# Two self attentions with the last values projected one step later, and a reordered end of the program, in a two-layer decoder on one core

## The chip, the cores and the metric

The kernel runs on one core of a Trainium2 chip. The metric is the device time of one execution in microseconds (us), the median of several runs. The engines are named as the profile names them: PE is TensorE (matmuls and transposes), PEld its weight loads, DVE VectorE, ACT ScalarE, POOL GpSimd, SP SyncE, which here issues nearly all transfers (SPq in the trace).

## The reference, cut to what matters

The input x has 8 batches of 128 tokens of 512 values. It goes through six blocks, each added to x and followed by a layer norm:

```
x = LN(x + attn0(x))            # 32 heads of 16, causal, biases
x = LN(x + autocorrelation(x, ctx))
x = LN(x + experts_lora(x))     # 28 experts, top 2
x = LN(x + attn1(x))            # 32 heads, clipped qkv, LN of q and k, ALiBi
x = LN(x + cross_attention(x, ctx))   # 16 heads, 4 groups of keys
x = LN(x + routed_lora(x))      # 8 heads of rank 16, softmax router
```

The change touches the two self attentions (`attn0`, `attn1`) and the last block of the last two pairs of batches. In an attention `v = x Wv` weighs nothing until the probabilities of its batch are known; only the product of probabilities and values needs it.

## The kernel before, in words

Everything is one program, with an instruction order written out by hand for every engine and semaphores between the engines. An engine takes its instructions strictly in that order.

**Self attentions.** Each of the two (`l` = 0 and 1) runs over steps `i`, four to a batch: batch `b = i // 4`, phase `r = i % 4`. The function `attention_step(l, i)` exists once for each engine. In every step PE makes the scores of step `i` twice: for the row maxima (into `s_bank`, L870, with the causal mask added on L844) and, five steps later and turned over, for the exponentials (into `t_bank`, L875). DVE reduces the first (`maxima`, L2134), ACT takes the exponential of the second (`probs`, L1406). PE's `scores(l, i)` waits for DVE's maxima of step `i - 1` and for ACT's exponentials of step `j - 1`, where `j = i - 5`. In the phases 1 and 3 PE multiplies probabilities and values (`weigh_values`, L891).

Beside these, the table `M_STEP` says which other product goes into which phase, and `M_BATCH` for which batch: phase 0 has the turned maxima, the rows of x, the output projection `o` and the transpose of q (`qT`); phase 1 has the projection of v of batch `b` and then the transpose of k of batch `b + 1` (`kT`, L829); phases 2 and 3 have the projections of q and k of batch `b + 2`, which the last two batches (6 and 7) no longer have. A projection is 12 matmuls of 512 columns (L749 to L751). All of them take turns in two banks of PSUM, `m_bank`; the order in `m_uses` decides which, and `bank_taken(u)` makes PE wait until the use before the last has been read.

After `kT`, ACT copies the turned keys into the ring `qk` (`qk_split`; one instruction for each of two halves in layer 0, L1374; eight smaller ones in layer 1, L1378). Then SP writes the extra rows of the keys and queries (`extra_rows`, L668, eight transfers), and PE's scores at the first step of the next batch (phase 0) wait for them. In its own order ACT has, in step `4b + 1`: `probs`, then the first half of a weight split (`split_hi`, L1339); in step `4b + 2`: `qk_split` of the keys, then `probs`. DVE takes v out of PSUM (`values`, L2089 in layer 0, L2091 in layer 1) at the head of the step behind the one that projects it. The turned maxima of a batch (L837) go to ACT and by SP's L659 into `qk`.

**End of the program.** Batches go in four trips of two (slots `s` = 0 and 1). The last block of trip 2 (`routes_and_low`, `low_to_rank`, `heads_out`) is woven into the cross attention of trip 3, and the last block of trip 3 stands alone at the end. All its products are in `bank[s][2]`: first 136 columns of router logits and low ranks (L1161), then the transpose (L1166), then 512 columns of output (L1172). DVE has `routes` (L2370 to L2372), `routed` (L2378 to L2380), `ff_add` (L2385) and `ff_moments` (L2390 to L2393); POOL makes rstd and shift (L1837, L1840); ACT applies them (`ff_norm`, L1613) and SP stores the batch when `ff_ready` says so. `norm_x_of_cross` (L2402) is the norm behind the cross attention, on DVE; `cross_add` is L2216 and `cross_moments` L2223 to L2227, with its rstd on POOL's L1826.

Of the kernel before, what the change touches and what calls it, by code (L numbers as in the profile page):

```python
# [109 lines left out]
def decoder(nc, a, out):  # L110
# [9 lines left out]
    with es:  # L120
# [174 lines left out]

        def bank_of_xv(trip, s, n):

            return bank[1][0] if (trip, s, n) == (0, 1, 0) else bank[s][3]
# [179 lines left out]
        M_STEP = (("max", "x", "o", "qT"), ("v", "kT"), ("q",), ("k",))  # L478
        M_BATCH = {"max": -1, "x": 2, "o": -3, "qT": 1, "v": 0, "kT": 1, "q": 2, "k": 2}

        def of_step(i, kind):

            b = i // STEPS + M_BATCH[kind]
            return b if kind in M_STEP[i % STEPS] and 0 <= b < B else None

        m_uses = {}
        for l in range(2):
            for i in range(FIRST, LAST):
                for kind in M_STEP[i % STEPS]:
# [125 lines left out]
        def _(sp):  # L615
# [18 lines left out]
            def store(trip, s):  # L634
                sp.wait_ge(ff_ready, row_of(trip, s))
# [108 lines left out]
        def _(pe):  # L744
# [411 lines left out]
            def routes_and_low(trip, s):  # L1156
# [3 lines left out]
                for k in range(KT):  # L1160
                    ins = mm(bank[s][2][:, 0:NL], plain_hT[:, k, s, 1, :], w_al[:, k, :], start=k == 0, stop=k == KT - 1)  # L1161
                ins.then_inc(mix_psum, 1)

            def low_to_rank(trip, s):
                pe.wait_ge(mixed_ready, mix(trip, s, FF))
                nc.tensor.transpose(bank[s][2][:, 0:P], low[s], ident[:, :]).then_inc(mixedT_psum, 1)  # L1166

            def heads_out(trip, s):
# [3 lines left out]
                mm(bank[s][2][:, :], plain_hT[:, KT - 1, s, 0, :], w_bl, start=True, stop=True).then_inc(ff_psum, 1)  # L1172
# [97 lines left out]
            for trip in range(TRIPS):  # L1270
# [26 lines left out]
                if behind:  # L1297
                    each(heads_out, trip - 1)
                cross_out(trip, 1, XKV - 1)
            x_to_features(TRIPS - 1, 0, FF, 1)  # L1300
            pe.wait_ge(ff_added, row_of(TRIPS - 2, 0))
# [3 lines left out]
            pe.wait_ge(ff_added, row_of(TRIPS - 2, 1))  # L1305
# [6 lines left out]
        def _(act):  # L1312
# [293 lines left out]
            def low_copied(trip, s):  # L1606
                act.wait_ge(mixedT_psum, mix(trip, s, FF))
                copy(plain_hT[:, KT - 1, s, 0, :], bank[s][2][:, 0:P]).then_inc(low_ready, 1)
# [126 lines left out]
            each(ff_norm, TRIPS - 1)  # L1735

        @block.gpsimd
        def _(pool):
# [95 lines left out]
            def ff_rows(trip, s):  # L1834
# [6 lines left out]
                                        ).then_inc(ff_rstd, 1)  # L1841

# [185 lines left out]
            each(ff_rows, TRIPS - 1)  # L2028

        @block.vector  # L2030
        def _(dve):
# [335 lines left out]
            def routes(trip, s):  # L2367
                dve.wait_ge(mix_psum, mix(trip, s, FF))
                e = st[s][:, EIGHT]
                steps_done(FF, trip, v.tensor_tensor(e, bank[s][2][:, LH * LR:NL], br_row[:, :], ALU.add))  # L2370
# [3 lines left out]
            def routed(trip, s):  # L2374
# [5 lines left out]
                v.tensor_tensor(low[s].rearrange("p (h r) -> p h r", h=LH), bank[s][2][:, 0:LH * LR].rearrange("p (h r) -> p h r", h=LH),  # L2380
                                e.unsqueeze(2).broadcast_to([P, LH, LR]), ALU.mult).then_inc(mixed_ready, 1)

            def ff_add(trip, s):
                dve.wait_ge(ff_psum, row_of(trip, s))
                v.tensor_tensor(xb(trip, s), bank[s][2][:, :], xb(trip, s), ALU.add).then_inc(ff_added, 1)  # L2385
# [9 lines left out]
            def each(step, trip, *args):  # L2395
                for s in both:
                    step(trip, s, *args)

# [115 lines left out]
            cross_moments(TRIPS - 1, 0)  # L2514
# [63 lines left out]
```

## Time and profile before

| | |
|---|---|
| median of 3 runs | 920.09 us (919.88 to 921.89) |
| profiled execution, own time | 921.42 us |
| its span, first to last instruction | 919.6 us |
| busy: PE, DVE, ACT, POOL | 855.2, 597.6, 419.6, 265.4 us |
| mean granted clock of TensorE | 0.98 |

The profiled execution is one run of the program; its span leaves out about 1.8 us around the first and last instruction, and its own time is 1.3 us above the median. A row of a timeline gives the start of an instruction (or of a few of the same kind), how long it took, its engine, line, operation and operands, and in brackets how long the engine sat idle before it and what it waited for. A row of a table of stretches gives the busy time of each engine in a stretch, the number of instructions, the granted clock (1.00 is full) and the share of the transfers.

### The profile page before, as it was taken

How to read it: one execution, taken by the hardware profiler on the slowest of the kernel's cores; microseconds unless marked ns; L12 is line 12 of the kernel's file. 1: busy time of each engine (PE TensorE's matmuls, PEld its weight loads, DVE VectorE, ACT ScalarE, POOL GpSimd, SP SyncE). 2: the span in 40 equal slices, each digit the busy share in tenths (PEclk: the TensorE clock that was granted, in tenths of full speed). 3: DMA queues.
4: the chain of work that ended last, by engine and by line, in shares of the span. 5: the costliest groups of instructions: out<-in, count | busy, mean ns of one | idle time of the engine just before them, and what ended most of it. 6: DMA issues, size and time to landing. Idle time of an engine off the chain costs nothing.

```text
span 919.6 us, 22457 instructions
## 1 busy us (share of the span) xinstructions
PE 855.2 (93%) x9192; PEld 692.4 (75%) x9192; DVE 597.6 (65%) x1526; ACT 419.6 (46%) x1078; POOL 265.4 (29%) x316
## 2 busy tenths in 40 slices
PE   6999998897997989899999798999999999999995
PEld 5777776674554777677777687888999898989983
DVE  3555665467896576567776543997377747665776
ACT  4354434344554334255555353543555364526532
POOL 1122222275985641101233246760000100010001
PEclk9999999999999999899999899999999999999998
DMA  6400000132231110000000011230000010000001
GB/s 225 159 20 15 20 16 23 60 93 81 80 100 36 46 40 4 9 27 17 17 17 17 26 36 57 88 122 8 24 1 2 1 47 1 2 2 24 2 2 46
DMA packets 21237, 37.11 MB, mean 40 GB/s; under 512 B 3264, under 2 KB 7488, under 8 KB 20880
## 3 DMA queue, kind: packets, MB, share of 16 engines
q1 hardware_dynamic: 21088, 35.62, 12.7%
q8 instruction: 73, 1.20, 0.5%
q14 instruction: 28, 0.23, 0.1%
q10 hardware_dynamic: 48, 0.07, 0.0%
HBM read 29.16 MB, written 2.10 MB: 34 GB/s over the span
## 4 chain that ended last, share of the span: by engine, by line
PE 73%; DVE 16%; issue 4%; POOL 2%; ACT 2%; DMA 2%; SPq 1%; POOLq 0%; DVEq 0%; ACTq 0%
PE bank L749 17%; PE bank L751 15%; PE bank L750 15%; PE bank L870 6%; PE bank L1142 4%; PE bank L891 3%; DVE tank L2348 3%; PE bank L844 2%; DVE tank L2358 2%; PE bank L875 2%; DVE tank L2263 1%; DVE tank L2134 1%; PE bank L829 1%; PE bank L1005 1%; PE bank L768 1%
## 5 line engine op out<-in xcount | busy, mean ns | idle before, releaser
L749 PE MATMUL bank<-wr,hTl 128*128 128x512 f32 (+3 forms) x472 | 190.6, 404 | 4.7 <-DVE wr L2063 2.3
L751 PE MATMUL bank<-wr,hTh 128*128 128x512 f32 (+3 forms) x472 | 181.5, 384 | 0.0
L750 PE MATMUL bank<-wr,hTh 128*128 128x512 f32 (+3 forms) x472 | 181.2, 384 | 0.0
L2134 DVE TENSOR_REDUCE tank<-bank 128x4 f32<-128x512 f32 x128 | 82.4, 686 | 57.0 <-PE bank L844 57.0
L749 PEld LDWEIGHTS bank<-wr,hTl 128*128 128x128 f32 (+1 forms) x472 | 90.3, 191 | 28.6 <-issue 8.6
L1406 ACT ACTIVATE pT<-bank 128x512 f32<-128x512 f32 x128 | 70.0, 605 | 88.1 <-PE bank L844 88.1
L751 PEld LDWEIGHTS bank<-wr,hTh 128*128 128x128 f32 (+1 forms) x472 | 90.0, 191 | 17.5
L750 PEld LDWEIGHTS bank<-wr,hTh 128*128 128x128 f32 (+1 forms) x472 | 90.4, 192 | 15.5 <-issue 1.2
L870 PE MATMUL bank<-qk 32*128 32x128 f32 x1024 | 75.5, 286 | 19.3 <-DVE tank L2134 8.8
L870 PEld LDWEIGHTS bank<-qk 32*128 32x128 f32 x1024 | 63.4, 188 | 35.9 <-issue 25.0
L875 PE MATMUL bank<-qk 32*128 32x128 f32 x1024 | 75.1, 285 | 0.3 <-DMA qk<-tank 0.3
L749 PE MATMUL bank<-hTh,wr 128*128 128x256 f32 (+1 forms) x240 | 73.3, 305 | 1.5 <-DVE hTl L2319 1.5
L751 PE MATMUL bank<-hTh,wr 128*128 128x256 f32 (+1 forms) x240 | 72.9, 304 | 0.0
L750 PE MATMUL bank<-hTl,wr 128*128 128x256 f32 (+1 forms) x240 | 72.9, 304 | 0.0
L1591 ACT ACTIVATE tank<-bank,stats 128x256 f32<-128x256 f32 x128 | 58.8, 482 | 23.2 <-DVE stats L2342 23.2
L875 PEld LDWEIGHTS bank<-qk 32*128 32x128 f32 x1024 | 62.7, 187 | 4.0 <-issue 3.0
L1378 ACT ACTIVATE qk<-bank,qk_shift,qk_scale 128x128 f32<-128x128 f32 x128 | 46.6, 474 | 24.7 <-PE bank L829 24.7
L2341 DVE TENSOR_REDUCE stats<-bank 128x2 f32<-128x512 f32 x64 | 43.8, 684 | 18.6 <-PE bank L751 18.6
L1837 POOL TENSOR_TENSOR stats<-stats,half 128x1 f32<-128x1 f32 x8 | 4.4, 550 | 175.4 <-DVE stats L2393 175.4
L2348 DVE COPY tank<-bank 128x512 f32<-128x512 f32 x64 | 39.7, 682 | 21.9 <-PE bank L1126 21.9
L1599 ACT CAST hTh<-bank 128x384 fp32r<-128x384 f32 x32 | 15.3, 479 | 83.4 <-PE bank L1142 83.4
L1142 PE MATMUL bank<-tank 128*32 128x128 f32 x1536 | 46.9, 280 | 2.8 <-DVE tank L2348 1.9
(238 smaller groups left out, 1854.3 us busy)
## 6 DMA issues: line engine op xcount, KB each, us to landing
raw<-w_qkv_dram SPq DMA_DIRECT2D x12, 256.0 KB, 2.9
raw<-w_xq_dram SPq DMA_DIRECT2D x16, 192.0 KB, 2.4
raw<-w_xo_dram SPq DMA_DIRECT2D x12, 256.0 KB, 2.8
x_all<-x_dram SPq DMA_DIRECT2D x8, 256.0 KB, 6.4
cin<-ctx_dram SPq DMA_DIRECT2D x8, 256.0 KB, 2.9
cin<-ctxT_dram SPq DMA_DIRECT2D x8, 256.0 KB, 2.9
out_dram<-x_all SPq DMA_DIRECT2D x8, 256.0 KB, 2.0
qk<-extra_dram SPq DMA_DIRECT2D x124, 16.0 KB
```

Of the source, the lines that this page charges most:

```text
L749: mm(dst, lhs[1], rhs[0], start=start, stop=False)
L750: mm(dst, lhs[0], rhs[1], start=False, stop=False)
L751: return mm(dst, lhs[0], rhs[0], start=False, stop=stop)
L870: ins = mm(s_bank[n][:, at], qk[b % RING][g, e, m, :], qk[b % RING][g, 2 + e, m, :], start=m == 0, stop=True, skip_group_check=True)
L875: ins = mm(t_bank[n][:, at], qk[c % RING][g, 2 + f, m, :], qk[c % RING][g, f, m, :], start=m == 0, stop=True, skip_group_check=True)
L1142: ins = mm(bank[s][0][row:row + NARROW, tile * P:(tile + 1) * P], xv[s][:, at:at + NARROW], xpT[s][:, (2 * j + t) * P:(2 * j + t + 1) * P] ...
L1378: ins = av(qk[b % RING][:, 2 * i + e, m, :], m_bank[u % 2][:, m * P:(m + 1) * P], ACT.Identity, bias=qk_shift[:, i, e, m:m + 1], scale=qk_ ...
L1406: av(pT[e][:, 2 * rows + n, :], t_bank[n][:, :], ACT.Exp).then_inc(exp_ready, 1)
L1591: ins = av(xp[s][:, h * XT:(h + 1) * XT], bank[s][i][:, j * XT:(j + 1) * XT], ACT.Exp, bias=st[s][:, NEGMAX.start + h:NEGMAX.start + h + 1 ...
L2134: v.tensor_reduce(nm[b % 2][:, at:at + KT], s_bank[n][:, :].rearrange("p (m t) -> p m t", m=KT), AX, ALU.max, negate=True).then_inc(max_re ...
L2341: steps_done(XA, trip, v.tensor_reduce(r, bank[s][i][:, :].rearrange("p (h t) -> p h t", h=2), AX, ALU.max))
L2348: v.tensor_copy(xpT[s][:, i * 512:(i + 1) * 512], bank[s][i][:, :]).then_inc(xpT_ready[s], 1)
```

## The change

In both self attentions, for batches 6 and 7 alone, phase 1 keeps only `kT` and the projection of v goes to phase 2, where these batches have nothing else; the use of the two banks follows that order, and DVE's `values` follows one step later.

At the end of the program, for trip 3 the products of the last block go to `bank[s][0]`. The two `heads_out` of trip 2, which stood before the output projection of slot 1 in the cross attention of trip 3, stand behind both output projections. PE's two waits for `ff_added` of trip 2 go. DVE's order is changed: slot 1 of the cross attention is added and measured before the `ff_add` of trip 2, and those and their moments are spread further back. The very last norm (trip 3, slot 1) goes from ACT to DVE, in the form with mean and rstd (`last_norm`), so POOL makes rstd alone for it (`ff_last`), and the last store waits for DVE.

```diff
+        def ff_bank(trip, s):
+            return bank[s][2] if trip + 1 < TRIPS else bank[s][0]
...
         M_STEP = (("max", "x", "o", "qT"), ("v", "kT"), ("q",), ("k",))
+        M_STEP_AT_END = (("max", "x", "o", "qT"), ("kT",), ("v",), ())
+        def kinds(i):
+            return (M_STEP_AT_END if i // STEPS in (B - 2, B - 1) else M_STEP)[i % STEPS]
...
-            return b if kind in M_STEP[i % STEPS] and 0 <= b < B else None
+            return b if kind in kinds(i) and 0 <= b < B else None
...
             def store(trip, s):
-                sp.wait_ge(ff_ready, row_of(trip, s))
+                if (trip, s) == (TRIPS - 1, 1):
+                    sp.wait_ge(ff_added, row_of(trip, s) + 1)
+                else:
+                    sp.wait_ge(ff_ready, row_of(trip, s))
...
                 cross_out(trip, 0, XKV - 1)
-                if behind:
+                if more and behind:
                     each(heads_out, trip - 1)
                 cross_out(trip, 1, XKV - 1)
+            each(heads_out, TRIPS - 2)
             x_to_features(TRIPS - 1, 0, FF, 1)
-            pe.wait_ge(ff_added, row_of(TRIPS - 2, 0))
             routes_and_low(TRIPS - 1, 0)
             x_to_features(TRIPS - 1, 1, FF, 1)
             low_to_rank(TRIPS - 1, 0)
-            pe.wait_ge(ff_added, row_of(TRIPS - 2, 1))
             routes_and_low(TRIPS - 1, 1)
...
             ff_norm(TRIPS - 2, 1)
-            each(ff_norm, TRIPS - 1)
+            ff_norm(TRIPS - 1, 0)
...
+            def ff_last(trip, s):
+                pool.wait_ge(ff_var, row_of(trip, s))
+                _, mv, rs, _ = ff_slots(trip)
+                nc.gpsimd.tensor_tensor(st[s][:, rs], st[s][:, mv][:, 1:2], half[:, 0:1], ALU.pow).then_inc(ff_rstd, 1)
...
             each(ff_rows, TRIPS - 2)
-            each(ff_rows, TRIPS - 1)
+            ff_rows(TRIPS - 1, 0)
+            ff_last(TRIPS - 1, 1)
...
+            def last_norm(trip, s):
+                _, mv, rs, _ = ff_slots(trip)
+                dve.wait_ge(ff_rstd, row_of(trip, s, 2, 1))
+                v.tensor_scalar(xb(trip, s), xb(trip, s), st[s][:, mv][:, 0:1], st[s][:, rs], ALU.subtract, ALU.mult).then_inc(ff_added, 1)
...
             cross_add(TRIPS - 1, 0)
             cross_moments(TRIPS - 1, 0)
+            cross_add(TRIPS - 1, 1)
+            norm_x_of_cross(TRIPS - 1, 0)
+            cross_moments(TRIPS - 1, 1)
             ff_add(TRIPS - 2, 0)
-            norm_x_of_cross(TRIPS - 1, 0)
+            norm_x_of_cross(TRIPS - 1, 1)
+            routes(TRIPS - 1, 0)
             ff_add(TRIPS - 2, 1)
-            cross_add(TRIPS - 1, 1)
-            cross_moments(TRIPS - 1, 1)
-            routes(TRIPS - 1, 0)
-            norm_x_of_cross(TRIPS - 1, 1)
             routed(TRIPS - 1, 0)
             ff_moments(TRIPS - 2, 0)
             routes(TRIPS - 1, 1)
+            ff_moments(TRIPS - 2, 1)
+            routed(TRIPS - 1, 1)
             ff_add(TRIPS - 1, 0)
-            routed(TRIPS - 1, 1)
-            ff_moments(TRIPS - 2, 1)
             ff_moments(TRIPS - 1, 0)
             ff_add(TRIPS - 1, 1)
             ff_moments(TRIPS - 1, 1)
+            last_norm(TRIPS - 1, 1)
```

## Rows read from the trace of the kernel before

**Rows 1.** Stretches of 6 and 5 us, layer 0 and layer 1, around step 28.

```profile
162.00:168.00 6.00, 5.88 (x60) 4.45 (x60) 1.29 (x2) 1.08 (x2) 0.00 (x0) 0.72 0.31 93
...
514.00:519.00 5.00, 5.00 (x51) 3.93 (x45) 1.29 (x2) 1.09 (x2) 0.00 (x0) 0.66 0.15 41
```

**Rows 2.** Timeline, layer 0, steps 25 to 28: PE, ACT, SP.

```profile
150.09 0.50 PE L749 MATMUL bank<-wr,hTl 128*128 128x512 f32 x1
...
153.00 0.60 PE L829 MATMUL bank<-ident,tank 128*128 128x128 f32 x4
...
156.32 0.38 PE L870 MATMUL bank<-qk 32*128 32x128 f32 x2 [1.28 <-DVE tank L2134]
...
162.12 0.38 PE L870 MATMUL bank<-qk 32*128 32x128 f32 x2 [2.69 <-DMA qk<-extra_dram]
...
153.63 1.45 ACT L1374 ACTIVATE qk<-bank,small_sb 128x512 f32<-128x512 f32 x2 [3.05 <-PE bank L829]
...
155.11 5.34 SPq L668 DMA_DIRECT2D qk<-extra_dram  x8
```

**Rows 3.** Timeline, layer 0, steps 29 to 32: DVE, PE.

```profile
173.59 0.76 DVE L2089 TENSOR_TENSOR tank<-bank,tank 128x256 f32<-128x256 f32 x2
...
176.13 0.88 DVE L2154 TENSOR_TENSOR tank<-tank,scratch 128x256 f32<-128x256 f32 x2
...
177.72 1.29 DVE L2134 TENSOR_REDUCE tank<-bank 128x4 f32<-128x512 f32 x2
...
176.27 0.38 PE L870 MATMUL bank<-qk 32*128 32x128 f32 x2 [1.28 <-DVE tank L2134]
...
179.06 0.33 PE L837 MATMUL bank<-ident,tank 128*128 128x128 f32 x1 [0.28 <-DVE tank L2134]
```

**Rows 4.** Timeline, layer 1, steps 25 to 28: PE, ACT, SP.

```profile
502.88 0.60 PE L829 MATMUL bank<-ident,tank 128*128 128x128 f32 x4
...
507.54 0.38 PE L870 MATMUL bank<-qk 32*128 32x128 f32 x2 [2.63 <-ACT pT L1406]
...
513.47 0.38 PE L870 MATMUL bank<-qk 32*128 32x128 f32 x2 [1.61 <-issue]
...
500.39 1.13 ACT L1406 ACTIVATE pT<-bank 128x512 f32<-128x512 f32 x2
501.34 0.57 ACT L1339 CAST wr<-raw 128x384 fp32r<-128x384 f32 x1
503.51 2.91 ACT L1378 ACTIVATE qk<-bank,qk_shift,qk_scale 128x128 f32<-128x128 f32 x8 [1.60 <-PE bank L829]
...
506.45 5.37 SPq L668 DMA_DIRECT2D qk<-extra_dram  x8
```

**Rows 5.** Timeline, end of the program, to the last routed low ranks: DVE, PE.

```profile
899.18 1.88 PE L1172 MATMUL bank<-raw,plain_hT 128*128 128x512 f32 x4
...
903.20 0.69 DVE L2216 TENSOR_TENSOR x_all<-bank,x_all 128x512 f32<-128x512 f32 x1
...
906.03 0.54 DVE L2402 TENSOR_SCALAR x_all<-x_all,stats 128x512 f32<-128x512 f32 x1
...
906.58 0.17 DVE L2378 RECIPROCAL stats<-stats 128x1 f32<-128x1 f32 x1
...
910.72 0.15 DVE L2378 RECIPROCAL stats<-stats 128x1 f32<-128x1 f32 x1
...
908.05 1.17 PE L1161 MATMUL bank<-raw,plain_hT 128*128 128x136 f32 x8 [0.33 <-ACT plain_hT L1322]
```

**Rows 6.** Timeline, end of the program, the last moments and norm.

```profile
912.39 0.68 DVE L2390 BATCH_NORM_STATS2 stats<-x_all 128x6 f32<-128x512 f32 x1
...
915.30 0.55 POOL L1837 TENSOR_TENSOR stats<-stats,half 128x1 f32<-128x1 f32 x1 [0.74 <-DVE stats L2393]
916.02 0.27 POOL L1840 TENSOR_SCALAR stats<-stats 128x1 f32<-128x1 f32 x1 [0.17 <-POOL stats L1837]
916.32 0.81 ACT L1613 ACTIVATE x_all<-x_all,stats 128x512 f32<-128x512 f32 x1 [0.92 <-POOL stats L1840]
```

More of the change, by code:

```diff
@@ L488, in decoder @@
             for i in range(FIRST, LAST):
-                for kind in M_STEP[i % STEPS]:
+                for kind in kinds(i):
                     if of_step(i, kind) is not None:
@@ L1160, in routes_and_low @@
                 for k in range(KT):
-                    ins = mm(bank[s][2][:, 0:NL], plain_hT[:, k, s, 1, :], w_al[:, k, :], start=k == 0, stop=k == KT - 1)
+                    ins = mm(ff_bank(trip, s)[:, 0:NL], plain_hT[:, k, s, 1, :], w_al[:, k, :], start=k == 0, stop=k == KT - 1)
                 ins.then_inc(mix_psum, 1)
@@ L1165, in low_to_rank @@
                 pe.wait_ge(mixed_ready, mix(trip, s, FF))
-                nc.tensor.transpose(bank[s][2][:, 0:P], low[s], ident[:, :]).then_inc(mixedT_psum, 1)
+                nc.tensor.transpose(ff_bank(trip, s)[:, 0:P], low[s], ident[:, :]).then_inc(mixedT_psum, 1)
             def heads_out(trip, s):
@@ L1171, in heads_out @@
                     pe.wait_ge(raw_loaded[1], loaded_piece(PIECES_REST + 1, 0, 0, PIECES_XV))
-                mm(bank[s][2][:, :], plain_hT[:, KT - 1, s, 0, :], w_bl, start=True, stop=True).then_inc(ff_psum, 1)
+                mm(ff_bank(trip, s)[:, :], plain_hT[:, KT - 1, s, 0, :], w_bl, start=True, stop=True).then_inc(ff_psum, 1)
             def each(step, trip, *args):
@@ L1607, in low_copied @@
                 act.wait_ge(mixedT_psum, mix(trip, s, FF))
-                copy(plain_hT[:, KT - 1, s, 0, :], bank[s][2][:, 0:P]).then_inc(low_ready, 1)
+                copy(plain_hT[:, KT - 1, s, 0, :], ff_bank(trip, s)[:, 0:P]).then_inc(low_ready, 1)
             def ff_norm(trip, s):
@@ L2369, in routes @@
                 e = st[s][:, EIGHT]
-                steps_done(FF, trip, v.tensor_tensor(e, bank[s][2][:, LH * LR:NL], br_row[:, :], ALU.add))
+                steps_done(FF, trip, v.tensor_tensor(e, ff_bank(trip, s)[:, LH * LR:NL], br_row[:, :], ALU.add))
                 steps_done(FF, trip, v.tensor_reduce(st[s][:, ONE_C], e, AX, ALU.max))
@@ L2379, in routed @@
                 steps_done(FF, trip, v.tensor_scalar(e, e, st[s][:, ONE_C], LH * 32.0 / LR, ALU.mult, ALU.mult))
-                v.tensor_tensor(low[s].rearrange("p (h r) -> p h r", h=LH), bank[s][2][:, 0:LH * LR].rearrange("p (h r) -> p h r", h=LH),
+                v.tensor_tensor(low[s].rearrange("p (h r) -> p h r", h=LH),
+                                ff_bank(trip, s)[:, 0:LH * LR].rearrange("p (h r) -> p h r", h=LH),
                                 e.unsqueeze(2).broadcast_to([P, LH, LR]), ALU.mult).then_inc(mixed_ready, 1)
@@ L2384, in ff_add @@
                 dve.wait_ge(ff_psum, row_of(trip, s))
-                v.tensor_tensor(xb(trip, s), bank[s][2][:, :], xb(trip, s), ALU.add).then_inc(ff_added, 1)
+                v.tensor_tensor(xb(trip, s), ff_bank(trip, s)[:, :], xb(trip, s), ALU.add).then_inc(ff_added, 1)
             def ff_moments(trip, s):
```

## The prediction

> **What bounds the kernel now.** I read the page first. PE is busy 855 of 919.6 us and is the last thing waited for nearly everywhere, so a stall counts only where PE stands idle, or where PE runs at half clock; the mean granted clock is 0.98, so that is rare. Then I went to the places of the change in the timeline, engine by engine, and looked for PE's idle time in brackets. It is in the steps that the change touches: batches 6 and 7 have no q or k to project in phases 2 and 3, so PE has nothing there but the scores, and waits for the answers to them. In layer 0 PE waits 1.28 us for DVE's maxima before the scores of step 27 and 2.69 us for the extra rows before those of step 28 [rows 2]; for batch 7 again 1.28 us before step 31, and 0.28 us before the turned maxima [rows 3]. In layer 1 it waits 2.63 us for ACT at step 27 and 1.61 us before step 28 [rows 4], where "issue" stands for the same transfers: SP issues them until 511.82, and 1.65 us later PE goes on, as in layer 0 (160.45 and 162.12). Last, the chain at the end of the program [rows 5, 6].
>
> **Layer 0, batch 6.** The keys' path to step 28 is a chain: the transposes start at 153.00, ACT copies 153.63 to 155.08, SP issues eight transfers in 5.34 us from 155.11, and PE starts step 28 at 162.12 [rows 2]: 9.1 us, none of it waiting for another engine. Now v stands behind it. v's twelve matmuls take from 150.09 to 153.00 [rows 2], so the chain starts 2.91 us earlier. Nothing else holds it: ACT and SP are idle then (ACT has waited 3.05 us for these transposes [rows 2]; the cast before it ends inside that wait), and the bank that the transposes now take is that of `o` of batch 3, read by DVE before v begins. PE has room to be ready at 159.2: it had 1.28 + 2.69 = 3.97 us of idle time, and v moves into it with 2.91. Term: 2.9 us. Bounds: 1.3 (only the maxima's wait is filled) and 4.0 (all idle time gone).
>
> **Layer 0, the clock.** Behind the 2.69 us wait the granted clock falls to 1.2 GHz, 0.72 on average over 162 to 168 [rows 1], while PE is busy 5.88 of 6 us. Lost: 6.0 x 0.28 = 1.7 us; the scores of step 28 are partly issue-bound, so I take 1.5. With about 1.3 us of idle time left, in two short pieces, that stretch looks like steps 29 to 32, where waits of 1.28 and 0.28 us [rows 3] were followed by no fall. Term: 1.5 us, bounds 0 and 1.7. The Trainium skill (TensorE: Matmul & The Clock Gate, "Loop structure matters more than you think") says that waiting for a DMA between matmuls makes the clock drop and that matmuls back to back keep it up; by that rule the stretch keeps its full clock, and the trace agrees in where the clock fell.
>
> **Batch 7, both layers.** No transpose here, only v moved from step 29 to 30. PE's 1.28 us wait before step 31 [rows 3] goes, since v lies between; a short new one comes before step 30, whose scores now follow `weigh_values` directly: the same sequence ends in 0.28 us before L837 [rows 3]. That would leave 1.0. But DVE is the next limit. It was free of step 29's work when it took v at 173.59 [rows 3]; now the maxima of step 30 start there and end at 174.9 (1.29). Then `weighed` for 1.6 us (176.13 to 177.72 [rows 3]), to 176.5, then v for 0.76, to 177.2, and only then the maxima of step 31, which PE's next instruction waits for. They started at 177.72 [rows 3]. Gain 0.5 to 0.7; I take 0.65 for each layer, bounds 0 and 1.28. In layer 1 the rows repeat this to 0.01 us. Queued behind DVE's delay are only later moments, with slack.
>
> **Layer 1, batch 6.** Transposes 2.91 us earlier again, from 502.88 to 499.97 [rows 4]. But ACT is not free: the exponentials of step 20 run until 501.52 and the cast `split_hi` until 501.91 [rows 4], and the keys' split is behind both in ACT's order. So it starts at 501.9 in place of 503.51, 1.6 earlier; from there to step 28 is 9.96 us (503.51 to 513.47 [rows 4]), so step 28 starts at 511.9. PE gets a new wait, for the exponentials before the scores of step 26: from 500.5 to 501.55, 1.0 us. It costs nothing by itself, as PE then comes to step 28 at 509.1 and still waits 2.8 us for the transfers. Term: 1.6 us, bounds 0.6 and 2.9. The clock was down before and behind step 28 (0.66 over 514 to 519 [rows 1], 5.0 x 0.34 = 1.7 us lost). As 2.8 us of waiting stay in front of the same place, I let this loss stand: term 0, bounds 0 and +1.7.
>
> **What follows** starts from those times: the transfers, splits and copies behind both attentions are released by the last steps' own results, none by something older that is still running. The values of both batches are needed only by `weigh_values` a step or more later, the wait for them on the bank's next user is over by then. So gains pass on whole.
>
> **The end.** The four matmuls of both `heads_out` of trip 2 (1.88 us as shown, 1.7 of them PE's alone [rows 5]) stood between the output projections and go behind the second, PE's sum unchanged. So DVE's add of slot 1 starts 1.7 earlier than 903.20, and its norm about 1.5 earlier than 906.03 [rows 5]. What is late next: `routed` of slot 0, which could start at 906.58 [rows 5] and now has an `ff_add` of 0.69 before it, from which 0.4 lies in idle time and 0.3 delays it. `low_to_rank` of slot 0 waits for it, and L1161 of slot 1 is behind that in PE's order: about 907.85 against 908.05 [rows 5]. Then trip 2's `ff_moments` of slot 1 (1.1 us, as 912.39 [rows 6] and the two small ones behind it) stands before `routed` of slot 1, which therefore starts at 910.65 against 910.72 [rows 5]. Of the 1.7 us, 0.1 stays. Behind that slot 0's add and moments end about 0.2 before the last `ff_add` needs DVE, so they cost nothing. The last norm: POOL's 0.55 stays; its second operation and ACT's 0.81, which ended at 917.13 [rows 6], give way to DVE's form of the same shape, 0.54 [rows 5], from 915.9 to 916.45. That is 0.65 to 0.7. The last store waits only for this; the one before it is issued 1.4 us earlier. The other bank and the two waits taken away are worth nothing: the wait seen there is for ACT's copy, 0.33 [rows 5]. Term: 0.75, bounds 0.3 (DVE's queue eats the rest) and 1.4 (the moved moments fall into idle time).
>
> **Sum.** 2.9 + 1.5 + 0.65 + 1.6 + 0.65 + 0.75 = 8.05 us. The profiled execution, 921.4, would come to 913.4; it is 1.3 above its median, so the median comes from 920.1 to 912.0.
>
> **Rivals.** (a) One half-clock stretch less: the one of layer 1 goes too; 910.4. For it: first idle 1.0, then 2.8, not 2.63 and 1.61. Against: 2.69 before the fall in layer 0. Chance 0.13. (b) The fall in layer 0 stays, or another comes in its place further on, for the autocorrelation has waits of its own; 913.5. Chance 0.17. (c) The transfers do not follow the transposes, because SP's or ACT's queue holds them: only the maxima's waits go, 1.3 + 0.65 in layer 0, 0.6 + 0.65 in layer 1, and 0.75: 4 us, 916. Against: SP is idle before both L668 rows. Chance 0.10. (d) The new waits eat it all, PE idles in other places by as much: 920. It needs a bound behind the attentions (weights, POOL) that I did not find. Chance 0.05. (e) Slower: everything behind step 25 shifts against the clock's control, and half-clock stretches fall on more busy places. Each costs up to 1.7 us [rows 1]; it decides from five net more, 8.05 / 1.7, and then gives 922. For it: waits of 1.0 and 2.8 us in layer 1 are new. Against: the mean clock is 0.98 in a program that already has waits of 1 to 3 us. Chance 0.04. The forecast itself has 0.51.
>
> **How the numbers follow.** The range reaches over (a) and (b) and into (c): 909 to 916. A change of 0.2% (1.84 us) is about what a measurement of this kernel can tell. Faster by more: the forecast, (a), (b), (c), 0.91; within it: (d), 0.05; slower: (e), 0.04.
>
> **What would show it.** In the changed profile: in layer 0 about 9.1 us from the transposes of the keys to step 28, a wait below 1.1 us before it and full clock behind it; layer 1's keys' split directly behind the cast L1339, a PE wait near 1 us before step 26 and near 2.8 us before step 28; before step 31 no wait, and DVE's v right before its maxima; at the end POOL's last operation followed by DVE's, then the store. Wrong if PE still waits over 2 us before step 28 in layer 0, if the autocorrelation takes longer than before by some us, or if the last norm ends less than 0.3 or more than 1.4 us earlier, counted from the last L1142.

## The result, and the profile after

The changed kernel takes 912.22 us (median of 10 runs, 908.46 to 916.69), the kernel before on the same chip 920.37 us (10 runs, 919.21 to 923.38): a ratio of 0.9904, 95% interval 0.9883 to 0.9925. The forecast was 912.0, in a range of 909 to 916. The profiled execution took 912.89 us (forecast 913.4), with a span of 911.1, 8.5 below that of before. So "faster" was right, and nearly to the microsecond; the steps behind the sum were not all of the size that they were given, and part of the agreement is luck: errors of about 1 us each that cancel. None of the signs that were to show the forecast wrong appeared.

In the code of after the lines named here stand 11 to 18 further down: L870 is L882, L837 is L849, L829 is L841, L875 is L887, L2134 is L2151, L2089 is L2106, L1172 is L1184. The first view is the timeline of the changed kernel in layer 0, steps 25 to 32, to be held beside [rows 2, 3]:

```profile
151.23 0.66 PE L841 MATMUL bank<-ident,tank 128*128 128x128 f32 x4
...
159.04 0.33 PE L849 MATMUL bank<-ident,tank 128*128 128x128 f32 x1 [0.27 <-DVE tank L2151]
160.42 0.38 PE L882 MATMUL bank<-qk 32*128 32x128 f32 x2 [1.05 <-DMA qk<-extra_dram]
...
164.85 0.38 PE L882 MATMUL bank<-qk 32*128 32x128 f32 x2
...
167.64 0.38 PE L882 MATMUL bank<-qk 32*128 32x128 f32 x2 [0.27 <-DVE tank L2151]
...
174.86 0.33 PE L849 MATMUL bank<-ident,tank 128*128 128x128 f32 x1 [0.27 <-DVE tank L2151]
...
151.93 1.45 ACT L1385 ACTIVATE qk<-bank,small_sb 128x512 f32<-128x512 f32 x2 [0.21 <-PE bank L841]
...
153.40 5.34 SPq L680 DMA_DIRECT2D qk<-extra_dram  x8
...
170.18 1.22 DVE L2151 TENSOR_REDUCE tank<-bank 128x4 f32<-128x512 f32 x2
...
172.87 0.71 DVE L2106 TENSOR_TENSOR tank<-bank,tank 128x256 f32<-128x256 f32 x2
173.51 1.29 DVE L2151 TENSOR_REDUCE tank<-bank 128x4 f32<-128x512 f32 x2
```

The turned keys leave PE at 151.23 and the scores of step 28 start at 160.42, 9.19 us later; the transfers take the same 5.34 us, and PE's wait is down from 2.69 to 1.05 us. The waits of 1.28 us before steps 27 and 31 are gone; 0.27 before step 30 (167.64) is new. DVE takes v at 172.87, directly behind `weighed`, and its maxima of step 31 follow at 173.51.

Layer 1, steps 25 to 32, beside [rows 4]:

```profile
494.17 0.66 PE L841 MATMUL bank<-ident,tank 128*128 128x128 f32 x4
495.85 0.38 PE L882 MATMUL bank<-qk 32*128 32x128 f32 x2 [1.02 <-ACT pT L1417]
...
503.07 0.33 PE L849 MATMUL bank<-ident,tank 128*128 128x128 f32 x1 [0.28 <-DVE tank L2151]
506.03 0.58 PE L882 MATMUL bank<-qk 32*128 32x128 f32 x2 [2.63 <-DMA qk<-extra_dram]
...
513.07 0.38 PE L882 MATMUL bank<-qk 32*128 32x128 f32 x2
...
515.86 0.38 PE L882 MATMUL bank<-qk 32*128 32x128 f32 x2 [0.27 <-DVE tank L2151]
...
523.08 0.33 PE L849 MATMUL bank<-ident,tank 128*128 128x128 f32 x1 [0.27 <-DVE tank L2151]
...
495.53 0.57 ACT L1350 CAST wr<-raw 128x384 fp32r<-128x384 f32 x1
495.93 2.97 ACT L1389 ACTIVATE qk<-bank,qk_shift,qk_scale 128x128 f32<-128x128 f32 x8
...
498.93 5.37 SPq L680 DMA_DIRECT2D qk<-extra_dram  x8
```

The keys' split stands right behind the cast, as forecast, with the new wait for ACT (1.02 us) and 2.63 us of waiting for the transfers. The clock is in the table of stretches (columns as in [rows 1]), three rows of after:

```profile
162.00:168.00 6.00, 5.73 (x104) 4.42 (x108) 3.55 (x6) 2.65 (x5) 0.00 (x0) 1.00 0.42 134
506.00:512.00 6.00, 5.97 (x56) 4.90 (x57) 1.29 (x2) 1.08 (x2) 0.00 (x0) 0.51 0.11 34
904.00:905.00 1.00, 1.00 (x2) 0.20 (x2) 0.82 (x3) 0.56 (x1) 0.02 (x1) 0.71 0.18 66
```

and one more of before, in layer 1, behind the wait of 2.63 us in front of step 27:

```profile
506.00:512.00 6.00, 4.32 (x81) 3.44 (x81) 2.89 (x6) 3.10 (x8) 0.30 (x1) 0.72 0.07 19
```

Behind layer 0's step 28 the granted clock stays at 1.00, where it was 0.72, and PE does 104 matmuls in 6 us instead of 60 [rows 1] (the same six microseconds, but not the same steps; step 28 itself took 4.43 us in place of 5.92). Behind layer 1's it is 0.51, the lower of the two levels (1.2 GHz) for nearly all of the six microseconds, deeper than the 0.66 of before [rows 1]. The third row is in the last product. The end of the program, beside [rows 5, 6]:

```profile
889.03 0.44 PE L1178 MATMUL bank<-ident,tank 128*128 128x128 f32 x2
...
898.25 0.68 DVE L2403 TENSOR_TENSOR x_all<-bank,x_all 128x512 f32<-128x512 f32 x1
898.85 0.15 DVE L2395 RECIPROCAL stats<-stats 128x1 f32<-128x1 f32 x1
...
902.42 0.15 DVE L2395 RECIPROCAL stats<-stats 128x1 f32<-128x1 f32 x1
...
908.04 0.55 DVE L2421 TENSOR_SCALAR x_all<-x_all,stats 128x512 f32<-128x512 f32 x1 [0.67 <-POOL stats L1857]
...
899.82 1.09 PE L1173 MATMUL bank<-raw,plain_hT 128*128 128x136 f32 x8
...
903.90 1.61 PE L1184 MATMUL bank<-raw,plain_hT 128*128 128x512 f32 x2 [0.35 <-ACT plain_hT L1619]
```

To book the difference, both traces are parted at the same instructions. Rows of before that are used for it and were not shown yet: step 29 in both layers, the turned maxima at the end of layer 1's attention, and two places in the tail.

```profile
168.04 0.38 PE L870 MATMUL bank<-qk 32*128 32x128 f32 x2
...
519.42 0.38 PE L870 MATMUL bank<-qk 32*128 32x128 f32 x2
...
530.44 0.33 PE L837 MATMUL bank<-ident,tank 128*128 128x128 f32 x1 [0.28 <-DVE tank L2134]
...
896.74 0.44 PE L1166 MATMUL bank<-ident,tank 128*128 128x128 f32 x2
...
912.21 1.13 PE L1172 MATMUL bank<-raw,plain_hT 128*128 128x512 f32 x2 [0.35 <-ACT plain_hT L1608]
```

| stretch | before | after | gain | forecast |
|---|---|---|---|---|
| start to the end of step 25's products of values, layer 0 | 150.09 | 151.23 | -1.1 | 0 |
| from there to step 28 | 12.03 | 9.19 | 2.8 | 2.9 |
| step 28 to the turned maxima, layer 0: clock | | | 1.5 | 1.5 |
| the same: v of batch 7 | | | 1.0 | 0.65 |
| to the same place of layer 1's step 25 (499.97; 494.17) | 320.9 | 319.3 | 1.6 | 0 |
| from there to step 28 | 13.50 | 11.86 | 1.6 | 1.6 |
| step 28 to the turned maxima, layer 1: clock | | | -1.1 | 0 |
| the same: v of batch 7 | | | 1.0 | 0.65 |
| to trip 2's last transposes (896.74; 889.03) | 366.3 | 365.95 | 0.35 | 0 |
| to the end of the last norm (917.13; 908.59) | 20.39 | 19.56 | 0.8 | 0.75 |

"Clock" and "v of batch 7" are parted at step 29: from step 28 to 29 layer 0 took 5.92 us before and 4.43 after, layer 1 5.95 and 7.04; from step 29 to the turned maxima both layers went from 11.02 to 10.01. The sum is 8.5 us. In the tail the last product starts 15.47 us behind the transposes before (896.74 to 912.21) and 14.87 after (889.03 to 903.90), but itself took 1.61 us against 1.13. Trip 2's transposes stand directly behind the last L1142, so the 0.8 us of the last row is also the distance that the forecast named for its end.

### The profile page after: what moved, and what is told of

Its sections match the earlier page's. It is cut to its first block, busy times and chain, and to the rows that moved or that the text cites. A ratio compares the mean times of both kernels' runs of the same rounds, so it can differ in the third digit from the quotient of the medians.

```text
span 911.1 us, 22453 instructions
## 1 busy us (share of the span) xinstructions
PE 852.5 (94%) x9192; PEld 689.2 (76%) x9192; DVE 599.0 (66%) x1527; ACT 418.0 (46%) x1077; POOL 264.9 (29%) x315
## 4 chain that ended last, share of the span: by engine, by line
PE 71%; DVE 17%; issue 4%; ACT 2%; DMA 2%; POOL 2%; SPq 2%; POOLq 0%; DVEq 0%; ACTq 0%
PE bank L761 17%; PE bank L762 15%; PE bank L763 15%; PE bank L882 6%; PE bank L1154 4%; DVE tank L2365 3%; PE bank L903 2%; PE bank L856 2%; DVE tank L2375 2%; PE bank L887 1%; DVE tank L2151 1%; PE bank L1017 1%; DVE tank L2280 1%; PE bank L841 1%; SPq L680 1%
## 5 line engine op out<-in xcount | busy, mean ns | idle before, releaser
L2151 DVE TENSOR_REDUCE tank<-bank 128x4 f32<-128x512 f32 x128 | 82.2, 683 | 52.6 <-PE bank L856 52.6
L882 PE MATMUL bank<-qk 32*128 32x128 f32 x1024 | 75.8, 286 | 13.9 <-DVE tank L2151 5.4
L882 PEld LDWEIGHTS bank<-qk 32*128 32x128 f32 x1024 | 63.7, 189 | 31.2 <-issue 23.6
L887 PE MATMUL bank<-qk 32*128 32x128 f32 x1024 | 75.2, 285 | 0.3 <-DMA qk<-tank 0.3
L887 PEld LDWEIGHTS bank<-qk 32*128 32x128 f32 x1024 | 62.9, 188 | 4.0 <-issue 3.0
L2375 DVE TENSOR_SCALAR tank<-tank,stats 128x256 f32<-128x256 f32 x128 | 47.6, 414 | 2.3
```

The source lines that it names most:

```text
L882: ins = mm(s_bank[n][:, at], qk[b % RING][g, e, m, :], qk[b % RING][g, 2 + e, m, :], start=m == 0, stop=True, skip_group_check=True)
L887: ins = mm(t_bank[n][:, at], qk[c % RING][g, 2 + f, m, :], qk[c % RING][g, f, m, :], start=m == 0, stop=True, skip_group_check=True)
L2151: v.tensor_reduce(nm[b % 2][:, at:at + KT], s_bank[n][:, :].rearrange("p (m t) -> p m t", m=KT), AX, ALU.max, negate=True).then_inc(max_re ...
L2375: ins = v.tensor_scalar(block, block, sums[:, j:j + 1], None, ALU.mult)
```

## The experiments

All ratios are to the kernel before, run on the same chip. Over all of them the kernel before had 75 runs, median 921.03 us, standard deviation 2.6; a median of 12 runs is therefore good to some 1 us, and the terms are read in the profiles as distances between two instructions, which repeat to 0.1 us where the clock is the same.

**The attentions alone.** The kernel before with the new table for batches 6 and 7, the end untouched.

```diff
+        M_STEP_AT_END = (("max", "x", "o", "qT"), ("kT",), ("v",), ())
+            return (M_STEP_AT_END if i // STEPS in (B - 2, B - 1) else M_STEP)[i % STEPS]
```

> Only the two self attentions are changed; the end of the program is that of the kernel before. Theory of the prediction: the gain is made of local terms, 2.8 (keys' path, layer 0) + 1.0 (batch 7, layer 0) + 1.6 (keys' path, layer 1) + 1.0 (batch 7, layer 1) = 6.4 us, and half-clock stretches move it by up to 1.7 us each either way: a median 5 to 8.5 us below the kernel before. In the profile, from the transposes of the keys of batch 7 to step 28: 9.2 us in layer 0 and 11.9 in layer 1. Rival (the gain is taken back behind the attentions by transfers and splits): under 3 us. Rival (the end does most of it): under 2 us.

Measured: 913.82 us (12 runs), 0.9922 (0.9893 to 0.9951). Layer 0 from the transposes of the keys to step 28 takes 9.14 us with a wait of 1.00, layer 1 11.89 us with 2.64, and the clock falls behind layer 1's step 28 as in the changed kernel (9.98 us from step 28 to 30, in full clock 7.2). So these distances belong to this half of the change, and most of the time does.

**Batch 7's v alone.**

```diff
-            return (M_STEP_AT_END if i // STEPS in (B - 2, B - 1) else M_STEP)[i % STEPS]
+            return (M_STEP_AT_END if i // STEPS in (B - 1,) else M_STEP)[i % STEPS]
```

> Only the values of batch 7 are projected one step later, in both layers; batch 6 and the end are those of the kernel before. Theory (each batch has its own wait): 1.0 us in each layer from the scores of step 29 to the turned maxima (11.02 us before, 10.0 here), the wait before step 28 stays at 2.69 us and the half clock behind it too; the median 2 us below the kernel before, plus or minus 1.5 for half-clock stretches. Rival (the gain is all that of batch 6, VectorE's queue bounds batch 7): under 0.5 us in the two stretches together.

Measured: 920.51 us, 0.9981 (0.9959 to 1.0004). Layer 0's waits at steps 27 and 28 are those of before (1.28 and 2.68 us), and in both layers the waits before step 31 are gone, with 10.0 us from step 29 to the turned maxima in place of 11.0. The local gain is 1.0 in each layer; the total, 0.6 us less, is at the low edge of what was expected and does not part the change from nothing.

**Batch 6's v alone.**

```diff
-            return (M_STEP_AT_END if i // STEPS in (B - 2, B - 1) else M_STEP)[i % STEPS]
+            return (M_STEP_AT_END if i // STEPS in (B - 2,) else M_STEP)[i % STEPS]
```

> Only batch 6's v is moved one step later, in both layers; batch 7's v and the program's end stay as before. Theory (the terms add up): L0 from the kT transposes to step 28 9.2 us instead of 12.0, the half clock behind step 28 gone (1.5), L1 from 13.5 to 11.9, a new half-clock stretch behind L1's step 28 (-1.1): 4.5 to 5 us in all, about 915.5. From the keys of batch 7 to the turned maxima the distance stays 11.0. Rival (batch 7's v, left where it was, gives part of it back, since its step starts earlier than its transfers land): L0's step 30 waits for the qk transfer, and the gain is 3 us or less, 917.5 or more.

Measured: 916.50 us (12 runs), 0.9945 (0.9922 to 0.9967): 4.9 us less. The timeline of this kernel, PE:

```profile
152.62 0.66 PE L834 MATMUL bank<-ident,tank 128*128 128x128 f32 x4
...
161.77 0.38 PE L875 MATMUL bank<-qk 32*128 32x128 f32 x2 [1.02 <-DMA qk<-extra_dram]
...
174.43 0.38 PE L875 MATMUL bank<-qk 32*128 32x128 f32 x2 [1.28 <-DVE tank L2139]
...
493.14 0.66 PE L834 MATMUL bank<-ident,tank 128*128 128x128 f32 x4
...
504.94 0.38 PE L875 MATMUL bank<-qk 32*128 32x128 f32 x2 [2.57 <-DMA qk<-extra_dram]
```

9.15 us in layer 0 and 11.80 in layer 1, the 1.28 before step 31 still there, and from step 28 to 31 12.66 us, against 14.15 before (162.12 to 176.27 [rows 2, 3]): 1.5 us is what the half clock behind the 2.69 us wait had cost. The rival, a wait at step 30 that eats part of it, did not come. Nor did the loss of 1.1 us that was expected behind layer 1's step 28: from there to step 29 it took 5.93 us, as before (5.95), though PE's wait was 2.57. So the distances add up to some 6 us, and the total has 4.9.

**The end alone**, that is, the changed kernel with the old table in both attentions.

```diff
-            return (M_STEP_AT_END if i // STEPS in (B - 2, B - 1) else M_STEP)[i % STEPS]
+            return (M_STEP_AT_END if False else M_STEP)[i % STEPS]
```

> Only the end of the program is changed, the attentions are those of the kernel before. Theory: 0.7 us from the last norm on VectorE and 0.1 to 0.6 from the order, a median 0.8 to 1.3 us below the kernel before, which is within what a measurement tells from nothing; in the profile 19.1 to 19.6 us from the last L1142-like product's transpose of the low ranks (trip 2) to the end of the last norm, against 20.39 before. Rival (the new order only shifts the queue on VectorE): 0.7 us or less, with the last heads_out no earlier.

Measured: 917.06 us, 0.9954 (0.9927 to 0.9981), 4 us less than the kernel before, where 0.8 to 1.3 were expected. The profile has only 1.3 of them at the end, 19.08 us from the transposes to the end of the norm in place of 20.39: the last product starts 14.88 us behind the transposes, as in the changed kernel, and the last norm is shorter. Up to the last 20 us the instructions are those of before, and layer 0's step 28 even was in half clock for longer (0.50 over 162 to 168, against 0.72 [rows 1]).

**The order of the end alone**: other bank and order, but the last norm on ACT as before.

```diff
-            last_norm(TRIPS - 1, 1)
...
-            ff_norm(TRIPS - 1, 0)
+            each(ff_norm, TRIPS - 1)
```

> The end of the program in its new order and with the other bank, but the last norm stays on ScalarE behind both GpSimd operations; attentions as before. Theory of the prediction: the order gives 0.1 us, the last norm 0.7, so this is 0.1 us below the kernel before. What the changed profile showed: the last heads_out starts 0.6 us earlier, counted from the transposes of trip 2's low ranks, so 0.6 us. Rival (the other bank matters by itself): a wait of TensorE for trip 2's adds appears nowhere in the kernel before, so nothing beyond the 0.6.

Measured: 919.97 us, 0.9972 (0.9950 to 0.9993). The last product again starts 14.87 us behind the transposes, 0.6 us earlier than before. Order, bank and the two waits taken away are not parted here.

**The last norm alone.** The kernel before with `ff_last` and `last_norm`, the old order and bank.

```diff
-            each(ff_norm, TRIPS - 1)
+            ff_norm(TRIPS - 1, 0)
...
-            each(ff_rows, TRIPS - 1)
+            ff_rows(TRIPS - 1, 0)
+            ff_last(TRIPS - 1, 1)
...
             ff_moments(TRIPS - 1, 1)
+            last_norm(TRIPS - 1, 1)
```

> Only the last norm goes from ScalarE to VectorE; the order of the end and all attentions as before. Theory: from the last sums on GpSimd to the end 0.7 us less, 919.7, a ratio of 0.999 whose interval can hold 1; the local distance in the profile decides. Rival (the gain of the two parts of the end comes only together, since the other bank is what frees VectorE): local distance unchanged.

Measured: 920.19 us, 0.9985 (0.9963 to 1.0007). From POOL's last operation (916.37) to the end of DVE's norm:

```profile
916.37 0.55 POOL L1849 TENSOR_TENSOR stats<-stats,half 128x1 f32<-128x1 f32 x1 [1.83 <-DVE stats L2402]
...
916.95 0.55 DVE L2412 TENSOR_SCALAR x_all<-x_all,stats 128x512 f32<-128x512 f32 x1 [0.67 <-POOL stats L1849]
```

1.13 us, against 1.83 before (915.30 to 917.13 [rows 6]). The 0.7 is there without the reordering, so the rival falls.

**The kernel before, again**, as a control of the comparison.

> The kernel before, unchanged, under another label: it measures what the comparison itself gives for no change. Theory (where the half-clock stretches fall differs from execution to execution, and the earlier single runs of the kernel before spread with a standard deviation of 2.6 us): a median within 2.5 us of the kernel before and an interval that holds 1. Rival (the comparison favours the kernel under test, so that part of the 8 us gained is not the change's): a median 3 us or more lower, a ratio below 0.997.

Measured: 920.93 us (12 runs), 1.0008 (0.9987 to 1.0030). The comparison favours nothing. In this execution the program's end was itself in half clock (0.73 over 904 to 909, where the first profile of before had 1.00), with no instruction changed.

**The changed kernel, again**, on the chip of the three that follow.

> The changed kernel itself, once more, beside the three built on it. Theory (half-clock stretches move the time from run to run): the single runs spread over 6 to 9 us, and within one kernel the longer runs are those with the lower mean clock, about 0.4 to 0.5 us for each us at half clock. The local stretches repeat to 0.1 us: 9.2 us and 11.9 us from the keys' transposes to step 28, 10.0 us from step 29 to the turned maxima. Rival (the spread comes from transfers): the runs' times have nothing to do with their clock.

Measured: 913.38 us (6 runs), 0.9928 (0.9901 to 0.9955). 9.16 us in layer 0; in layer 1 11.78, a wait of 2.54 and the same fall behind it (10.09 us from step 28 to 30).

**The wait filled.** Does layer 1's fall come from the wait for the transfers? Ten matmuls whose result nobody reads are put in front of step 28's scores in layer 1, into a bank that is free; the kernel computes all else as before.

```diff
+                if l == 1 and i == STEPS * (B - 1):
+                    u = m_uses[l, "o", b - 3]
+                    bank_taken(u)
+                    for _ in range(10):
+                        mm(m_bank[u % 2][:, :], w_qkv1[0][:, 0, 0:P], w_qkv1[0][:, 0, 0:D], start=True, stop=True)
                 scores(l, i)
```

> The changed kernel, with ten more matmuls of 512 columns in layer 1 between the turned maxima and the scores of step 28, written to a bank that the output projection overwrites: work without use, 2.3 us, inside the wait of 2.63 us. Theory (the half clock behind the wait comes from the wait): step 28 starts where it did, 11.9 us after the keys' transposes, and runs at full clock, 4.4 us to step 29 in place of 7.0; a median 1.5 to 2.6 us below the changed kernel although more is computed. Rival (the clock falls there for another reason, or falls later instead): step 28 as long as before, or the same sum with the fall in another place; then the time is that of the changed kernel. Rival (a cost of the added work): 0.2 us later.

Measured: 910.60 us (6 runs), 0.9899 (0.9879 to 0.9918). The timeline of PE and the table of stretches:

```profile
504.34 2.54 PE L932 MATMUL bank<-wr 128*128 128x512 f32 x10
507.18 0.38 PE L882 MATMUL bank<-qk 32*128 32x128 f32 x2 [0.31 <-issue]
...
514.41 0.38 PE L882 MATMUL bank<-qk 32*128 32x128 f32 x2 [0.27 <-DVE tank L2156]
```

```profile
507.00:513.00 6.00, 5.82 (x108) 4.62 (x108) 1.98 (x3) 1.09 (x2) 0.00 (x0) 1.00 0.13 37
```

Step 28 starts no earlier (11.84 us behind the transposes), but the clock behind it is 1.00 and step 30 follows 7.23 us later, in place of 9.83 (506.03 to 515.86). The fall did not move elsewhere nearby either: from 490 to 532 us the granted clock is 1.00 throughout. The fall was the wait's, and cost 2.6 us in this place. The medians on the same chip, 910.60 against 913.38, go the same way, though six runs of each would not show it alone. More work, less time.

**Two queues.** The eight transfers are issued one after another by SP in 5.3 us. Here, for the last batch, ACT's queue issues four of them, beside SP's four.

```diff
-                    if (l, b, e) != (0, 0, 0):
+                    if (l, b, e) != (0, 0, 0) and (b, e) != (B - 1, 1):
...
+                if i == STEPS * (B - 2) + 2:
+                    act.wait_ge(qk_rows, batch(l, B - 1, 2, 2))
+                    for g in range(GROUPS):
+                        at = g * PAD + 1
+                        act.dma_start(qk[(B - 1) % RING][at:at + 4, 1:4:2, :, :], a["extra"][l, 1, g]).then_inc(extra_loaded[1], 16)
```

> The changed kernel, but four of the eight transfers of the extra rows of batch 7 are issued by ScalarE, behind its exponentials of step 26, in both layers. Theory (what TensorE waits for at step 28 is the issue time of eight transfers one after another): the wait of 1.05 us in layer 0 goes, that of 2.63 us in layer 1 falls to about 0.6, step 28 starts 1.0 and 2.0 us earlier counted from the keys' transposes, and as the long wait is gone so is the half clock behind it in layer 1 (1.5 to 2.6 us): a median 3 to 5.5 us below the changed kernel. Rival (the waits are the landing time of the transfers or the split on ScalarE): less than 0.5 us in either layer. Rival (ScalarE's issue delays its exponentials and these TensorE): a new wait before step 27 or 29.

Measured: 905.97 us (4 runs, 903.61 to 907.86), 0.9848 (0.9824 to 0.9872), which is 7.4 us below the changed kernel on that chip, more than the expected 3 to 5.5. And once more, the same code:

> The changed kernel with the qk transfers of the last batches issued half on SyncE's queue and half on ScalarE's, the same code as the run at 905.97 us. Theory (the wait for the transfers behind the keys' transposes goes, 1.0 us in layer 0 and 2.0 in layer 1, and with it the half clock behind layer 1's step 28): 904 to 908 us, a ratio of 0.982 to 0.988. Rival (the earlier value was low because its half-clock stretches fell well by chance): 909 to 912, as the changed kernel less the local 3 us at most.

Measured: 910.82 us (6 runs, 905.41 to 911.38), 0.9875 (0.9848 to 0.9903), in the rival's range and not in the expected 904 to 908. So the first value was, in part at least, luck: by the clocks of the single runs, its four spent 24.9 us each at the lower level, the six of the second 31.5. The two were taken on different chips, and their intervals overlap. The timeline of the second, layer 0 and layer 1, and its stretch:

```profile
151.89 0.66 PE L841 MATMUL bank<-ident,tank 128*128 128x128 f32 x4
...
159.69 0.33 PE L849 MATMUL bank<-ident,tank 128*128 128x128 f32 x1 [0.27 <-DVE tank L2156]
159.95 0.38 PE L882 MATMUL bank<-qk 32*128 32x128 f32 x2
...
154.05 2.88 SPq L680 DMA_DIRECT2D qk<-extra_dram  x4
...
497.01 0.66 PE L841 MATMUL bank<-ident,tank 128*128 128x128 f32 x4
...
506.73 0.38 PE L882 MATMUL bank<-qk 32*128 32x128 f32 x2 [0.48 <-DMA qk<-extra_dram]
...
513.95 0.38 PE L882 MATMUL bank<-qk 32*128 32x128 f32 x2 [0.27 <-DVE tank L2156]
```

```profile
506.00:512.00 6.00, 5.51 (x89) 4.31 (x93) 1.98 (x3) 1.62 (x4) 1.27 (x1) 1.00 0.14 39
```

SP issues in 2.88 us what took 5.34; layer 0's step 28 comes 8.06 us behind the transposes without a wait for the transfers, layer 1's 9.72 us with 0.48, and the clock behind both is full. Locally that is 1.1 + 2.1 + 2.6 = 5.8 us less than the changed kernel. All ten runs of it have a median of 908.84 us, the sixteen of the changed kernel 912.88: a difference of 4.0 us, and it beats both kernels.

**Two queues, and the cast later.** The first half of layer 1's weight split stands before the keys' split on ACT; here, for step 25, it goes one step later, behind the keys' split and the exponentials, and ACT issues three transfers, SP five. The lines of the transfers are left out below.

```diff
-                if r == 1 and 0 <= b < B:
+                late = i - 1 if l == 1 and i in (STEPS * (B - 2) + 1, STEPS * (B - 2) + 2) else i
+                if (r == 1 and late == i or r == 2 and late < i) and 0 <= b < B:
                     split_hi(pieces(b // 2), b % 2, b // 2, 2, before)
```

> As the kernel with two queues, but five transfers are issued by SyncE and three by ScalarE, and in layer 1 ScalarE's weight cast of step 25 stands behind the keys' split and the exponentials of step 26. Theory (the keys' path is split, issue, landing, each behind the other): another 0.3 to 0.4 us earlier in layer 1 at the split, 11.9 us from the transposes to step 28 becomes 9.5 or less, so there is hardly a wait before step 28; a median 3.5 to 6 us below the changed kernel. Rival (the cast delayed holds the weights back later): a wait for weights behind the attention of layer 1 that the changed kernel does not have.

Measured: 909.34 us (6 runs), 0.9884 (0.9859 to 0.9909). PE and SP in layer 1:

```profile
504.88 0.50 PE L761 MATMUL bank<-wr,hTl 128*128 128x512 f32 x1 [0.83 <-POOL hTl L1802]
...
497.27 3.64 SPq L680 DMA_DIRECT2D qk<-extra_dram  x5
```

Layer 1 took 9.65 us from the transposes to step 28, where 9.5 or less was expected and 9.72 is the value with the cast in its place. The keys' split did start 0.4 us earlier behind the transposes (1.37 us in place of 1.77), but SP's issuing took 3.64 us in place of 3.01, so its last transfer went out no earlier. The two edits are not parted, and what the later cast gives with four transfers on either queue was not tried. Its price shows: 8.12 us (502.55 to 510.67) from step 28 to 30 in place of 7.22, with a new wait of 0.83 us, before the output projection, for a half of the attention's values (`hTl`) that POOL makes; in POOL's order it stands behind POOL's half of the weight split, which waits for the cast. The cast can't be delayed for nothing.

## Why the prediction came out right, point by point

**Layer 0, batch 6: right.** 2.84 us against 2.9, from one chain moved whole; alone (9.15 us) and in the changed kernel (9.19 and 9.16) it is the same. The rest of the wait, 1.05, is within what was said.

**Layer 0, the clock: right.** 1.5 us, and 1.00 over the stretch. The filled wait shows the mechanism in layer 1 by a direct test. The Trainium skill (TensorE: Matmul & The Clock Gate, "Loop structure matters more than you think") has matmuls back to back keep the clock up and a wait for a DMA between them lower it; the trace agrees with both halves, 1.00 with the wait filled and 0.51 with the wait.

**Batch 7: right mechanism, size too small.** I put 0.65 per layer and it gave 1.0. The step that was off is "DVE is the next limit ... now the maxima of step 30 start there", at 173.59. Counted from step 29's scores (168.04 before, 164.85 after), the maxima of step 30 started at 5.33 and not at the 5.55 where v had been taken, since they start right behind DVE's reciprocal; and maxima, multiplication, turn and v behind them took 3.33 (170.18 to 173.51) and not 3.6, as the rows' durations overlap by 0.05 to 0.1 us each. So the maxima of step 31 start at 8.66, where I had 9.16 and before had 9.68 (177.72 [rows 3]): 1.0 gained. That is the 1.0 that I had named as PE's own share, 1.28 less 0.27, and it is no coincidence: the maxima of step 31 start 1.44 us behind that step's first scores (172.07), as they do at step 27 (156.25 to 157.69), where DVE waits for the scores. So DVE only just keeps up, and PE's own order sets the distance, not DVE's queue.

**Layer 1, batch 6: right.** 1.64 against 1.6, with the cast as the limit and a new wait of 1.02 (forecast 1.0). In the experiment with the later cast the split does start 0.4 us earlier, which bears out the cast as the limit.

**Layer 1, the clock: wrong by 1.1.** The step that failed is "I let this loss stand". The wait did stay, 2.63, but the loss grew from 1.5 to 2.6 us (0.51 over the stretch instead of 0.66). The time at the lower level did not grow, it is some 7 us in both; its place changed. Before, one half of it (0.72 over 506 to 512) lay behind the wait in front of step 27 and cost nothing, as PE then waited 1.61 us for the transfers all the same; the other half (0.66 over 514 to 519) lay behind step 28. After, the wait in front of step 27 is gone, and nearly all of it (0.51 over 506 to 512, the rest in the wait of 2.63) lies behind step 28, where PE has no slack. Why one wait is followed by so long a fall is open, and it differs between profiles: it was so in three of the four in which batch 6's v is moved and the wait is left (the changed kernel twice, the attentions alone); with batch 6 alone it was half of that, 0.75 over 506 to 512, and cost 1.5. Of the six profiles in which batch 6 is as before, all have a fall behind the wait of 2.6 us in front of step 27, and five have one behind step 28, too. The sixth, with the last norm alone, has none there, although PE waited 1.65 us (12.66 us from step 28 to 31, against 14.18). This was neither rival (a) nor (e) but of their kind: one stretch more on a busy place.

**The end: right sum by luck, the order off.** The last norm gave 0.7 (forecast 0.65 to 0.7). The order gave 0.6 and not 0.1. The step that failed is that `routed` of slot 0 has an `ff_add` of 0.69 before it, of which "0.3 delays it": DVE's add ran at 898.25 while ACT still made the exponentials, and the reciprocal at 898.85 came no later behind the transposes than before (9.82 us against 9.84). PE's products of slot 1 then start right behind the transpose of slot 0 (899.82) instead of waiting for ACT, 0.5 us earlier (10.79 against 11.31 behind the transposes), and that gain is not eaten by the moments of trip 2, which I had in front of `routed` of slot 1: they take the place of an `ff_add` that had waited for PE's product, and the reciprocal starts 1.47 us behind the first operation of `routes` in both (909.25 to 910.72, 900.95 to 902.42). The half-clock stretch inside the last product (0.71 at 904) took 0.5 back, so the total looked like my 0.75. The end experiments have 14.87 and 14.88 us for the same distance.

**What follows: passed on whole, but for the clock.** Outside the places of the change the profile has -1.1, +1.6 and +0.35 us. They are no work of the change's: the instructions there are the same. The first is half clock, 28 to 36 us with 1.00 before and 0.79 after. The 1.6 us come in at two places (208 to 226 and 280 to 295 us of before), at which the two traces have their half-clock stretches beside different instructions; over the whole stretch the mean clock is 0.97 in both, so that the places and not the amount make the difference is likely, and not shown. Rival (d), a bound behind the attentions, did not show, nor did (c).

**What the totals say.** Each run has a span and a mean clock, and (1 - clock) x 2 x span is its time at the lower level: on average 39.1 us before, 39.2 in the control, 34.5 with batch 6 alone, 31.4 in the changed kernel, 28.8 with two queues. Over 197 runs, with one constant for each kernel, a run is 0.36 +/- 0.02 us longer for each such microsecond. By that 2.8 of the 8.7 us between the means of the changed kernel (16 runs) and of before (75) are clock, 5.9 are not. The end alone had 32.7 us of it, 6.4 less than before: 2.3 of its 3.5 us, and the other 1.2 are the 1.3 of the profile. Why a kernel that differs only in its last 20 us has fewer of these microseconds is not settled; the 6.4 have a standard error of 1.9, and the control speaks against the comparison as a reason. Also open is that the part without clock (5.9 us; 2.7 with batch 6 alone) is nearly 2 us less than the local distances add up to (7.8 and 4.5); the 0.36 is an average over places where half clock costs more and less.

## What to carry to other kernels

Where the path to PE's next work runs through a chain of copy, issue and landing, put the work that feeds nobody soon behind the head of the chain; the chain's own rows give the gain to 0.1 us. Count a wait on PE twice: once as idle time and once as the half clock that may follow it. Here half clock cost nothing where PE would have waited anyway, and 1.5 to 2.6 us where PE had no slack; ten useless matmuls could buy it back. Eight small transfers in a row on one queue were 5.3 us of issuing here; splitting them over two brought step 28 another 1.1 and 2.1 us nearer, and is worth trying before anything else is moved. And a total of a dozen runs resolves 1 us here at best, so judge a part of a change by the distance between two instructions of the profile.

## What the runs showed of the hardware

That one program has its half-clock stretches at different places from run to run, 39 us of them on average, and that most of its spread of 2.6 us goes with this, as the instructions are the same: with the clock taken into account the spread is 1.3. A median of few runs can be lucky by 3 us (905.97 and 910.82 for the same code). A wait of 2.5 to 2.7 us for the transfers, or for ACT, was followed by half clock in every profile, one of 1.0 us in layer 0 in none (12.66 us from step 28 to 31 with batch 6 alone), and one of 1.6 to 1.9 us before layer 1's step 28, some 6 us behind one of 2.6, in five of six. The fall lasted twice as long in some profiles (0.50 and 0.51 over 6 us) as in others (0.72 and 0.75). Eight transfers issued from one queue took 0.67 us each, and PE went on 1.65 to 1.75 us behind the last of them.
